# Dense attentions: own source for the constant rows, first head pair straight from the part buffers, four sum buffers, and one normalisation moved

## The reference

```python
# layer 0, per batch element: softmax over keys, rotary q and k
q, k, v = split(x @ qkv_w + qkv_b);  q, k = rotary(q), rotary(k)
x = x + softmax(q @ k.T * 8 ** -0.5) @ v @ out_w + out_b
# layer 1: the input is normalised; each weight exp(s) is gated by sigmoid(s - mu) and renormalised
h = layernorm(x)
x = x + weights(h @ Wq + bq, h @ Wk + bk, mu) @ (h @ Wv + bv) @ Wo + bo
```

## Time and profile before

| | |
|---|---|
| median of the runs | 4421.68 us |
| the profiled execution | 4406.58 us, of which 4404.8 us are the span of its instructions |
| mean granted TensorE clock | 0.88 |
| PE / DVE / ACT / POOL busy | 76% / 63% / 58% / 31% |
| first attention's stage begins | 408.4 us |
| norm stage before the second attention | 1230.8 to 1254.6 us |
| second attention's stage begins | 1254.6 us |

### The profile page before, as it was taken

The page is one execution under the profiler, slowest core; times in us unless marked ns, Lnnn a source line. Parts: engine busy times, 40 slices in busy tenths (PEclk is TensorE's granted clock), DMA queues, the critical chain, the costliest instruction groups (busy, mean ns, idle before and its releaser), DMA issues. The chain is left out here.

```text
span 4404.8 us, 53696 instructions
## 1 busy us (share of the span) xinstructions
PE 3349.2 (76%) x20182; PEld 1501.4 (34%) x20182; DVE 2760.8 (63%) x4514; ACT 2544.5 (58%) x4198; POOL 1352.1 (31%) x1221
## 2 busy tenths in 40 slices
PE   7597788989948988988887897899868696631126
PEld 4365122222211222222212565466544273211124
DVE  5123889989736665665565776477667132488886
ACT  2022377767858989989996776377533222312225
POOL 0401184010011010010001885388411403228880
PEclk9699799999979999999998999899989898775558
DMA  4101121110020010000000111011020021550000
GB/s 135 34 19 56 30 50 34 33 31 16 2 62 15 15 26 18 15 18 12 15 1 16 28 35 36 14 34 35 17 81 8 31 64 32 77 62 0 10 6 24
DMA packets 140026, 137.36 MB, mean 31 GB/s; under 512 B 42185, under 2 KB 104693, under 8 KB 139765
## 3 DMA queue, kind: packets, MB, share of 16 engines
q1 hardware_dynamic: 130612, 116.07, 12.0%
q0 software_dynamic: 8192, 16.79, 1.6%
q10 hardware_dynamic: 960, 1.05, 0.1%
HBM read 64.90 MB, written 33.82 MB: 22 GB/s over the span
## 5 line engine op out<-in xcount | busy, mean ns | idle before, releaser
L460 PE MATMUL PS<-t 50*128 50x512 bf16 (+2 forms) x3072 | 739.4, 398 | 187.6 <-ACT t L603 49.5
L722 DVE TENSOR_TENSOR t<-t 128x1536 f32<-128x1536 f32 (+1 forms) x384 | 586.3, 1596 | 129.7 <-ACT t L603 77.7
L585 ACT ACTIVATE t<-PS 128x512 f32<-128x512 f32 x1024 | 532.5, 602 | 230.9 <-PE PS L460 227.5
L640 DVE TENSOR_REDUCE t<-PS 128x1 f32<-128x1024 f32 x512 | 601.0, 1216 | 46.3 <-PE PS L452 42.3
L534 PE MATMUL PS<-t 128*9 128x512 f32 x4096 | 552.5, 612 | 12.6 <-DVE t L722 12.1
L605 ACT ACTIVATE t<-PS 128x1536 f32<-128x1536 f32 (+1 forms) x384 | 477.9, 1310 | 51.1 <-PE PS L460 35.9
L603 ACT ACTIVATE t<-PS 128x1536 f32<-128x1536 f32 (+1 forms) x384 | 476.9, 1310 | 37.4 <-PE PS L460 25.5
L460 PEld LDWEIGHTS PS<-t 50*128 50x128 bf16 (+2 forms) x3072 | 158.7, 94 | 970.8 <-ACT t L603 270.5
L452 PE MATMUL PS<-t 48*128 48x512 bf16 x1024 | 342.8, 406 | 47.2 <-DVE t L640 24.5
L1801 POOL TENSOR_TENSOR t<-t 128x512 f32<-128x512 f32 x128 | 159.7, 1269 | 576.6 <-ACT t L1666 576.1
L2617 PE MATMUL PS<-t 128*128 128x32 f32 x256 | 61.1, 403 | 344.6 <-ACT t L2663 280.9
(11 more groups left out here) (403 smaller groups left out, 6385.1 us busy)
## 6 DMA issues: line engine op xcount, KB each, us to landing
t<-scr SPq DMA_DIRECT2D x336, 64.0 KB
t<-t SPq DMA_DIRECT2D x128, 128.0 KB, 2.3
scr<-t SPq DMA_DIRECT2D x96, 128.0 KB
t<-t SPq DMA_DIRECT2D x16, 512.0 KB, 13.1
scr<-t SPq DMA_DIRECT2D x2, 2560.0 KB
t<-scr SPq DMA_DIRECT2D x16, 320.0 KB, 3.6
scr<-t SPq DMA_DIRECT2D x16, 320.0 KB, 2.7
t<-scr SPq DMA_DIRECT2D x48, 48.0 KB
```

Of the source, the lines that this page charges most:

```text
L460: return e.op.matmul(PS[:, bk, :], Kx[p // 4 % 2][lo:lo + rows, j, kb * 128:kb * 128 + 128], Qx[p // 4 % 2][lo:lo + rows, j, hf * 512:hf * ...
L585: e.op.activation(P[x % 4][:, 2 * hf + side, :], PS[:, bank((what, p, k, side, hf)), :], ACT.Exp, scale=S8).then_inc(*PW.up((p, k, side, hf)))
L640: e.op.tensor_reduce(MX[p % 2][:, side, qc:qc + 1], PS[:, 2 * side:2 * side + 2, :].rearrange("p a n -> p (a n)"), AX, ALU.max).then_inc(* ...
L722: e.op.tensor_tensor(o, o, SGM[(12 * p + 3 * blk + ti) % 3][:, 0:nu, :], ALU.mult).then_inc(*DG.up((p, blk, ti)))
```

## The change

- **Constant rows.** Their sources are now in P[3] (`consts`), a tile that is first written by the exponentials. They are sent behind the part sends of batch element 0: in the first attention behind the fetch of pairs 1 to 3, in the second before it. Minus mu is made behind v. ACT no longer waits for them before its first cast, but before it first writes P[3] (`third_free`).
- **First pair.** Its rows go from the part buffers in SBUF to Qx and Kx by `first_rows`, six DMAs for each half of q and of k on SP (side 0) and six on ACT (side 1), each of 8 rows of 512 tokens. That is 24 on each queue instead of 12 DMAs of 8 rows of 1024 tokens out of scratch memory. ACT's are put between its casts. SP's writes of the parts to scratch, which the later fetches read, stand behind its small DMAs but for the first three.
- **Four sum buffers** instead of two, so the wait of VectorE for GpSimd is gone. k's parts lie in P[3].
- **Rows for later.** L1369 is removed; VectorE makes the 32 chunks of XN in the opening of the second attention, behind minus mu (`first_norm`), and GpSimd's bias addition waits for that.

```diff
@@ -273,7 +273,7 @@
...
 
-def attention(first, wq, wk, wv, bq, bk, bvb, wo, extra, load, row, mix=None):
+def attention(first, wq, wk, wv, bq, bk, bvb, wo, extra, load, row, mix=None, also=None):
@@ -313,10 +313,12 @@
...
     MIN = [sig("max_in0"), sig("max_in1")]
-    HEAD0 = sig("first_pair_in")
-    first_parts = (part, [[P[1 + x][:, y, 0:256].bitcast(BF16) for y in range(3)] for x in range(2)])
-    QS = (QF, P[0][:, 0, :])
-    RS = (R1, P[0][:, 1, :])
+    HEAD0 = [sig("first_pair_in0"), sig("first_pair_in1")]
+    first_parts = (part, [[P[3][:, y, 256 * x:256 * x + 256].bitcast(BF16) for y in range(3)]
+                          for x in range(2)])
+    consts = [P[3][0:3, y, 0:256].bitcast(BF16) for y in ((3,) if first else (4, 5, 6, 7))]
+    QS = ((QF, P[0][:, 0, :]), (P[0][:, 2, :], P[1][:, 0, :]))
+    RS = ((R1, P[0][:, 1, :]), (P[0][:, 3, :], P[1][:, 1, :]))
@@ -415,17 +417,31 @@
...
         else:
-            e.wait_ge(HEAD0, 0)
-
-    def fetch_first(e, side):
-
-        e.wait_ge(SENT[0], (0, 1, 0))
-        e.wait_ge(SENT[1], (0, 1, 1))
-        for qi, rank in enumerate(((0, 0, 0, 1, 1, 2), (0, 1, 2, 0, 1, 0))):
-            for j, p3 in enumerate(rank):
-                lo = 64 * side + 8 * j
-                e.op.dma_start((Qx, Kx)[qi][0][lo:lo + 8, 0, :],
-                               qD[qi, 0, p3, 64 * side:64 * side + 8, :]).then_inc(*HEAD0.up(0, 16))
+            for side in range(2):
+                e.wait_ge(HEAD0[side], 0)
+
+    RANKS = ((0, 0, 0, 1, 1, 2), (0, 1, 2, 0, 1, 0))
+
+    def first_rows(e, side, qi, hf):
+
+        e.wait_ge(PO, ("split", 0, qi, hf))
+        for j, p3 in enumerate(RANKS[qi]):
+            lo, ns = 64 * side + 8 * j, slice(512 * hf, 512 * hf + 512)
+            e.op.dma_start((Qx, Kx)[qi][0][lo:lo + 8, 0, ns],
+                           first_parts[qi][hf][p3][64 * side:64 * side + 8, :]).then_inc(*HEAD0[side].up(0, 16))
+
+    def const_rows(e):
+
+        e.wait_ge(DV, "ones")
+        for u in range(2):
+            for lo in (KP, 64 + KP):
+                for x, (dst, src, n) in enumerate(
+                        ((Kx, consts[0], 2),) if first else
+                        ((Kx, consts[0], 1), (Kx, consts[1], 1), (Kx, consts[2], 1), (Qx, consts[3], 3))):
+                    at = lo + x % 3
+                    e.op.dma_start(dst[u][at:at + n, :, :].rearrange("p h (a n) -> p (h a) n", a=2),
+                                   src[0:n, :].unsqueeze(1).broadcast_to([n, 8, 512])).then_inc(
+                        *ONES.up("ones", 16))
@@ -560,25 +576,33 @@
...
         n = 0
+
+        def third_free(e):
+
+            e.wait_ge(ONES, "ones")
+            e.wait_ge(SENT[0], (0, 1, 0))
+            e.wait_ge(SENT[1], (0, 1, 1))
...
                 e.wait_ge(DV, ("sum", qi, hf))
-                if qi == 0 and (not first or hf == 0):
-                    e.wait_ge(ONES, "ones")
-                e.op.copy(first_parts[qi][hf][0][:], QS[hf][:]).then_inc(*AC.up(("high", qi, hf)))
+                e.op.copy(first_parts[qi][hf][0][:], QS[qi][hf][:]).then_inc(*AC.up(("high", qi, hf)))
...
                 e.wait_ge(DV, ("less", qi, hf))
-                e.op.copy(first_parts[qi][hf][1][:], QS[hf][:]).then_inc(*AC.up(("middle", qi, hf)))
-            elif what == "fetch" and i[0] == 0:
-                fetch_first(e, 1)
+                e.op.copy(first_parts[qi][hf][1][:], QS[qi][hf][:]).then_inc(*AC.up(("middle", qi, hf)))
+                if qi or hf:
+                    first_rows(e, 1, (2 * qi + hf - 1) // 2, 1 - hf)
+                if qi and hf:
+                    first_rows(e, 1, 1, 1)
...
                     e.wait_ge(PV, ((x - 4) // 8, (x - 4) % 8))
+                elif x == 3:
+                    third_free(e)
@@ -599,6 +623,8 @@
...
                         e.wait_ge(PV, (p - 1, 2 * blk + 1))
+                    elif blk == 3 and ti == 0:
+                        third_free(e)
@@ -615,13 +641,10 @@
...
             return e.op
-        if first:
-            e.op.memset(part[0][0][0:2, :], 1.0).then_inc(*DV.up("ones"))
         e.op.memset(PS[:, PVB, :], 0.0).then_inc(*DV.up("zeroed"))
-        if not first:
-            e.op.memset(part[1][0][0:3, :], 1.0).then_inc(*DV.up())
-        loaded(e)
-        if not first:
+        e.op.memset(consts[-1][0:2 if first else 3, :], 1.0).then_inc(*DV.up("ones"))
+
+        def minus_mu():
@@ -630,8 +653,9 @@
...
             for x in range(3):
-                e.op.tensor_copy(part[0][x][0:1, :], parts[0:1, x:x + 1].broadcast_to([1, 512])).then_inc(
+                e.op.tensor_copy(consts[x][0:1, :], parts[0:1, x:x + 1].broadcast_to([1, 512])).then_inc(
                     *DV.up("ones"))
+        loaded(e)
@@ -646,19 +670,17 @@
...
                 if b == 0:
-                    if qi:
-                        e.wait_ge(PO, ("split", 0, 0, hf))
...
                         e.op.scalar_tensor_tensor(
-                            out=(QS, RS)[x][hf][:], in0=src, scalar=bb,
+                            out=(QS, RS)[x][qi][hf][:], in0=src, scalar=bb,
...
                         if x:
-                            then().tensor_tensor(QS[hf][:], QS[hf][:], RS[hf][:], ALU.add).then_inc(
+                            then().tensor_tensor(QS[qi][hf][:], QS[qi][hf][:], RS[qi][hf][:], ALU.add).then_inc(
...
                     else:
-                        e.op.tensor_scalar(QS[hf][:], src, bb, None, ALU.add).then_inc(
+                        e.op.tensor_scalar(QS[qi][hf][:], src, bb, None, ALU.add).then_inc(
@@ -675,8 +697,12 @@
...
                 e.wait_ge(AC, ("high", qi, hf))
-                e.op.tensor_tensor(QS[hf][:], QS[hf][:], first_parts[qi][hf][0][:], ALU.subtract).then_inc(
-                    *DV.up(("less", qi, hf)))
+                e.op.tensor_tensor(QS[qi][hf][:], QS[qi][hf][:], first_parts[qi][hf][0][:],
+                                   ALU.subtract).then_inc(*DV.up(("less", qi, hf)))
+            elif what == "fetch" and i[0] == 0 and not first:
+                minus_mu()
+            elif what == "bias" and also:
+                also(e)
@@ -776,6 +802,8 @@
...
                 loaded(e)
+                if also:
+                    e.wait_ge(DV, "also")
@@ -789,12 +817,15 @@
...
                     pt = first_parts[qi][hf]
-                    e.op.tensor_tensor(pt[2][:], QS[hf][:], pt[1][:], ALU.subtract).then_inc(
+                    e.op.tensor_tensor(pt[2][:], QS[qi][hf][:], pt[1][:], ALU.subtract).then_inc(
...
                     then().tensor_tensor(QF[:], QF[:], R1[:], ALU.add).then_inc(*PO.up())
+                if b == 1:
+                    for side in range(2):
+                        e.wait_ge(HEAD0[side], 0)
@@ -808,44 +839,36 @@
...
             load(e)
-        if first:
-            e.wait_ge(DV, "ones")
-            for x in Kx:
-                for lo in (KP, 64 + KP):
-                    e.op.dma_start(x[lo:lo + 2, :, :].rearrange("p h (a n) -> p (h a) n", a=2),
-                                   part[0][0][0:2, :].unsqueeze(1).broadcast_to([2, 8, 512])).then_inc(
-                        *ONES.up("ones", 16))
-        else:
-            e.wait_ge(DV, "ones")
-            for u in range(2):
-                for lo in (KP, 64 + KP):
-                    for x in range(3):
-                        e.op.dma_start(
-                            Kx[u][lo + x:lo + x + 1, :, :].rearrange("p h (a n) -> p (h a) n", a=2),
-                            part[0][x][0:1, :].unsqueeze(1).broadcast_to([1, 8, 512])).then_inc(
-                            *ONES.up("ones", 16))
-                    e.op.dma_start(Qx[u][lo:lo + 3, :, :].rearrange("p h (a n) -> p (h a) n", a=2),
-                                   part[1][0][0:3, :].unsqueeze(1).broadcast_to([3, 8, 512])).then_inc(
-                        *ONES.up("ones", 16))
+
+        def send_parts(b, qi, hf):
+            pt = part[hf] if b else first_parts[qi][hf]
+            for p3 in range(3):
+                e.op.dma_start(qD[qi, b, p3, :, 512 * hf:512 * hf + 512], pt[p3][:]).then_inc(
+                    *SENT[hf].up((b, qi, hf), 16))
...
                 b, qi, hf = i
+                if b == 0:
+                    first_rows(e, 0, qi, hf)
+                    if qi == 0 and hf == 0:
+                        send_parts(0, 0, 0)
+                    elif qi and hf:
+                        for qh in ((0, 1), (1, 0), (1, 1)):
+                            send_parts(0, *qh)
+                        if not first:
+                            const_rows(e)
+                    continue
                 e.wait_ge(PO, ("split", b, qi, hf))
-                pt = part[hf] if b else first_parts[qi][hf]
-                for p3 in range(3):
-                    e.op.dma_start(qD[qi, b, p3, :, 512 * hf:512 * hf + 512], pt[p3][:]).then_inc(
-                        *SENT[hf].up((b, qi, hf), 16))
+                send_parts(b, qi, hf)
...
                 own = 0 if u else 1
-                if u == 0:
```

(15 more changed lines are left out.)

## The result

| | before | after |
|---|---|---|
| median | 4421.94 us (20 runs, 4412.2 to 4444.3) | 4405.1 us (20 runs, 4390.7 to 4417.0) |
| ratio | | 0.9958 [0.9949, 0.9968], so 18.6 us |
| span of the profiled execution | 4404.8 | 4408.8 |
| first attention, from its stage's start to its end | 822.5 | 834.4 |
| of it, start to first maximum | 31.6 | 29.65 |

The changed kernel is faster, but by 16.8 us (difference of the medians) to 18.6 us (the ratio) instead of 24. The profiled execution of after is not faster at all: it lost 11.9 us in the first attention although its opening gained 2.0, and 7.1 us in a later stage whose code is the same in both kernels (296.6 to 303.7).

The account below looks back on a forecast made before the run. Stages run in a row, so critical-path savings come off the whole; both openings wait on serial chains ending in DMAs. -8.6 - 3.1 - 12.5 = -24.2 us takes 4421.7 to 4397.5; own range 4390 to 4404, 8-in-10 range 4381 to 4412.

Parts of the forecast that it names:

- Norm stage, -8.63: End of the double norm: without the 32 ACT operations VectorE ends the stage at 1245.72 instead of ACT at 1254.35.
- Moved normalisations hidden: Second opening: the 32 VectorE operations, 8.4 us, lie under the opening's DMAs and the first tiles.
- the rival of 4405.9: Second attention: the moved normalisations are not covered and make VectorE late for the gated tiles, +8.4 us; chance 0.05.
- First opening, -3.1: Start of the first attention: ACT's last direct-row issue starts at 434.6 and lands at 436.9, against TensorE's old start at 440.01.
- Second opening, -12.5: Start of the second attention: first tile 26.1 us after the stage's start, against 38.6 before.
- Cheap issue: Both openings: 8-row DMAs go out at 0.37 us each, -37.2 us in all, 4384.5; chance 0.15.
- issue next to free: Both openings: issue costs next to nothing and arithmetic bounds the queues, -48.6 us in all, 4373; chance 0.03.
- late landing: Both openings: 48 small DMAs back up, landing 9.1 us from issue instead of 2.3, -10.6 us in all, 4411; chance 0.12.
- Added wait of ACT, counted 0, up to 3: Second attention: ACT's tenth tile waits for the constant rows, landing about level with the need; 0, up to 3 us.
- The clock as the slower rival: Second attention's first tiles: the low clock grant stays on, +53 us over two head pairs, 4450; chance 0.03.
- the fetch behind the opening hidden: First attention: SP's next fetch, its 24 issues ending at 447, is first needed at 463, so it costs nothing.

Follow-up runs that it names:

- the wide rows: Changed kernel with the later fetch, its direct rows sent as 24 DMAs of 1024 tokens instead of 48: ratio 0.9868, on a slower chip 0.9908.
- the late fetch: Changed kernel with the first attention's fetch of the next four head pairs put two steps later, behind the sending of the row maxima: ratio 0.993.
- the two runs on the normalisations: Kernel before with only the 32 normalisations moved to VectorE: ratio 0.998; changed kernel with them put back on ACT: 4405.94 us, 0.9984 (9.8 us above the changed kernel).
- the scratch path with the same waits removed: Changed kernel with only the direct rows undone, the first pair's rows fetched from scratch memory again: 4239.15 against 4259.12 us on the same chip, ratio 0.992.

## Why the prediction was right, and where it was off

4405.1 us lies in the wide range (4381 to 4412) and on the side of "faster", 7.6 above the forecast of 4397.5. It lies just outside the forecast's own range (4390 to 4404), to which 0.62 had been given, and next to the 4405.9 of a rival that the traces don't bear out. So the direction and the main terms were right, and that the total was so near is in part luck: several terms were off, and the two attentions were read only up to their first products.

- **Norm stage, -8.63:** right. 15.2 for 23.8 us in every trace; 8.5 us taken alone, 9.8 undone.
- **Moved normalisations hidden** (the rival of 4405.9): right up to the first tile. They end at 1281.13, 0.35 before the first tile of after, and without them the tile comes no earlier. Whether they cost some 3 us behind it is open.
- **First opening, -3.1:** measured -2.0 in the traces compared; over all traces the first maximum is at 29.5 to 29.65 us with the change and at 30.5 to 31.7 without. ACT's queue ends 27.2 us after the stage's start, against 26.9 worked out, by two errors that cancel: an issue took 0.74 us instead of 0.64, and the casts that the prediction put between the issues ran beside them. SP's queue, which was to end at 24.4, ends last, at 27.5. And TensorE begins 2.8 us behind the start of its last issue, not 2.3.
- **Second opening, -12.5:** -11.8 in the first trace, -10.2 to -11.4 in the others (first tile at 27.2 to 28.4 for the same code). The step that failed is SP's queue, which was to end at 23.1, ahead of ACT's. It has the same 24 issues at 0.74 and three sends of 1.95 us in all between them, and ends 25.5 us after the start, 1.8 behind ACT's. (At the prediction's own prices, 24 of 0.64 and three of 0.43 from 7.0 on, it would have ended at 23.7.) The landing was shorter than counted, 1.8 us in every trace of this code. What differs from trace to trace is when SP's first issue goes out, 5.8 to 7.3 us after the start.
- **Cheap issue, issue next to free, late landing:** out. An issue took 0.74 with the gap, not 0.37, and TensorE began 1.8 to 2.8 us behind the last one's start, not 9.
- **Added wait of ACT, counted 0, up to 3:** ACT waits 1.5 to 1.6 us there in all traces of this code, for SP's queue was late by that. The tenth tile starts 16.9 to 17.0 us behind the first, against 15.4 in the kernel before; but in other traces with the old opening it is at 14.3 to 16.9, held up by TensorE, so the wait is not always a loss.
- **The clock as the slower rival:** its sign, a grant of 0.50 beyond 13 us after the first tile, did appear: 15.5 us in after. But it was set too tight to tell the kernels apart, for the kernel before had 13.4 us in the trace compared, and 11.1 to 18.3 in the other traces with its opening, against 16.0 to 18.0 in those of after. The longest, 25.3 us in a trace of the wide rows, came with a loop that was 5.8 us longer, not 53.
- **What no step had: the loops.** The prediction called the fetch behind the opening hidden because its rows are needed late. That holds for the rows; what it did not look at is who stands behind the fetch on the same queue, the rows of maxima, for which TensorE waits. That wait was in the trace of before (10.6 us), and the changed opening leaves it there, perhaps by 6 us longer. And of the 11.8 us by which the first tile of the second attention came earlier, only 7.7 are left at that stage's end: its loop took 1098.8 us instead of 1094.7. The other traces give 1097.4 and 1098.5 for this code (1092.5 with the late fetch) and 1093.9, 1094.3 and 1098.0 for the old opening, so this part isn't settled either.

For the stages that the change touches, the means over the traces with the early fetch (for the second attention, without the two runs on the normalisations) are -8.6 for the norm stage, +4.2 for the whole first attention and -6.9 for the whole second, -11.3 us in all; the timed runs show 12 to 19. So it is known where the sum was too good (the end of SP's queue in both openings, and both loops at nothing), but how the missing 7.6 us divide among them is open.

The reading also missed the larger lesson: the direct rows, whose opening was forecast faster than the old one, are slower than the scratch path with the same waits removed. The prediction had priced both (0.37 and 0.64 an issue, 12 and 24 of them) and did not compare them with each other, only each kernel as a whole.

## What to carry to other kernels

Price a shortcut against the old path with its other waits gone, not against the old path as it ran: 24 direct issues of 0.74 us lost to a round trip whose 12 issues cost 0.36. When a queue gets a batch of DMAs, list what small transfers stand behind it and who waits for them; one condition that let a row go ahead of a batch was worth about as much as this whole change. And before a difference between two traces is explained, look at how far two traces of one kernel differ in the same stage (here 818 to 830 us for one code of the first attention, in four traces).

## What was unexpected of the hardware

- Issuing an SBUF-to-SBUF DMA of 8 rows took 0.67 to 0.69 us at the median, with 1 KB or 2 KB a row, on SP's and on ACT's queue; the same rows out of scratch memory took 0.30 to 0.32:

```profile
L432 ACTq DMA_DIRECT2D t<-scr x24: 275/317/633, 361.7 to 1187.7; - x24
L432 SPq DMA_DIRECT2D t<-scr x24: 285/296/352, 361.7 to 1187.5; - x24
```

- A small write behind a batch of 24 DMAs was on its way for 3.8 to 15.6 us, from one execution to the next by another amount; with the batch behind them instead, the same writes took 1.3 to 3.2, most of them under 1.6.
- Two chips ran the kernel before in 4271 and 4272 us and a third in 4414, with the difference in a few stages only. Why is open.
